# Four instruction lists of a software pipeline laid in a new order, and one wait of VectorE left out

## What is computed

```
h = jnp.maximum(_layernorm(x, axis=-1), 0.0)
x = x + _L0_gnn_ref(h, adj, ...)   # 4-head graph attention, a 1-head one, a feed-forward net, layernorm
h = jnp.maximum(_layernorm(x, axis=-1), 0.0)
x = x + _L1_gnn_ref(h, adj, ...)   # masked self-attention with 8 heads
h = jnp.maximum(_layernorm(x, axis=-1), 0.0)
x = x + _L2_gnn_ref(h, adj, ...)   # deg * (h @ Wi + b) + adj @ (h @ Wj)
h = jnp.maximum(_layernorm(x, axis=-1), 0.0)
x = x + _L3_gnn_ref(h, adj, ...)   # 1-head graph attention beside its own projection
```

## Time and profile before

| | before |
|---|---|
| median of 3 runs | 2682.44 us (2681.39 to 2683.78) |
| the profiled execution: its own time | 2683.62 us |
| its span, first to last instruction | 2681.8 us |
| mean granted clock of PE | 0.987 |
| PE busy | 2580.8 us, 96% of the span |
| PE's weight loads (PEld) busy | 2333.0 us, 87% |
| DVE busy | 2304.7 us, 86% |
| ACT busy | 2061.2 us, 77% |
| POOL busy | 1248.4 us, 47% |

### The profile page before, as it was taken

How to read it: one execution, slowest core, us unless ns; L and a number is a source line. 1 busy time by engine, 2 the same in 40 slices (tenths; PEclk the granted TensorE clock), 3 DMA queues, 4 the chain that set the end, 5 groups by cost and what they waited for, 6 DMA issues and landing times.

```text
span 2681.8 us, 64380 instructions
## 1 busy us (share of the span) xinstructions
PE 2580.8 (96%) x21761; PEld 2333.0 (87%) x21761; DVE 2304.7 (86%) x8352; ACT 2061.2 (77%) x5708; POOL 1248.4 (47%) x2015
## 2 busy tenths in 40 slices
PE   4899999999999999999999999999999999999985
PEld 3789999998998998999999999899999899999874
DVE  5689889889888888888888888888988988988884
ACT  4688788787787887877877877878878878878752
POOL 3545445444444444454454454454544544544431
PEclk9999999999999999999999999999999999999986
DMA  4000000000000000000000000000000000000000
GB/s 131 1 2 9 17 17 9 17 17 14 13 17 13 13 17 17 10 17 17 10 17 17 10 17 17 10 17 17 9 17 17 9 17 17 10 17 13 9 9 12
DMA packets 41286, 44.29 MB, mean 17 GB/s; under 512 B 2816, under 2 KB 40448, under 8 KB 40832
## 3 DMA queue, kind: packets, MB, share of 16 engines
q1 hardware_dynamic: 40816, 39.14, 4.6%
q10 hardware_dynamic: 144, 1.05, 0.1%
HBM read 23.40 MB, written 16.78 MB: 15 GB/s over the span
## 4 chain that ended last, share of the span: by engine, by line
PE 70%; ACT 20%; POOL 4%; issue 3%; DVE 2%; SPq 1%; DMA 0%; ACTq 0%; DVEq 0%; POOLq 0%
PE pA L1084 12%; PE pB L1191 11%; PE pE L1084 7%; PE pB L1158 7%; PE pB L1084 7%; ACT probs L579 7%; PE pF L1315 4%; PE pC L1084 3%; ACT pA L573 3%; ACT B_h_high L613 2%; PE pF L1328 2%; PE pA L1302 2%; PE pC L1237 2%; ACT C_hid_t L649 2%; ACT whs L560 1%
## 5 line engine op out<-in xcount | busy, mean ns | idle before, releaser
L677 ACT ACTIVATE F_s_t<-F_s_t,F_m 128x128 f32<-128x128 f32 x1024 | 325.3, 395 | 0.9 <-DVE F_m L863 0.8
L1191 PE MATMUL pB<-wout_high,B_h_high 128*128 128x258 f32 x1024 | 307.4, 300 | 1.1 <-DVE B_h_low L897 1.1
L1191 PE MATMUL pB<-wout_low,B_h_high 128*128 128x258 f32 x1024 | 289.6, 283 | 0.0
L1191 PE MATMUL pB<-wout_high,B_h_low 128*128 128x258 f32 x1024 | 288.8, 282 | 0.0
L1158 PE MATMUL pB<-probs,whs 128*128 128x128 f32 x2048 | 285.4, 282 | 1.4 <-ACT wh L620 1.1
L1158 PEld LDWEIGHTS pB<-probs,whs 128*128 128x128 f32 x2048 | 254.2, 192 | 20.8 <-issue 2.4
L1084 PE MATMUL pA<-wh_high,A_hT_high 128*128 128x512 f32 x512 | 229.0, 447 | 9.5 <-POOL wh_low L388 8.4
L889 DVE SCALAR_TENSOR_TENSOR B_e<-B_e,pB 128x512 f32<-128x512 f32 x256 | 172.9, 675 | 71.7 <-ACT B_e L605 71.4
L464 POOL TENSOR_TENSOR B_h_low<-B_e,B_h_high 128x512 fp32r<-128x512 f32 x128 | 165.8, 1295 | 111.8 <-ACT B_h_high L613 111.8
L1084 PE MATMUL pA<-wh_high,A_hT_low 128*128 128x512 f32 x512 | 202.9, 396 | 0.0
L1084 PE MATMUL pA<-wh_low,A_hT_high 128*128 128x512 f32 x512 | 202.7, 396 | 0.0
...
## 6 DMA issues: line engine op xcount, KB each, us to landing
...
```

The lines of the kernel that those rows point to most:

```text
L677: last = act.activation(F_s_t[:, s, h, :], F_s_t[:, s, h, :], ACT.Exp, scale=-1.0, bias=F_m[:, s, h:h + 1])
L1191: last = pe.matmul(pB[:, 0, 0:D + 2], a, w[:, k, :], start=(k == 0 and i == 0), stop=(k == KH - 1 and i == 2))
```

## The change

The four lists are written anew, and `x_there` loses its wait for `A_moments`. No computation is added, taken away or cut differently. Most steps keep their place in the pipeline and move by some places in the list; the lists also begin at another step, which by itself changes nothing. The diff (of the lists, which are tables, a line of each):

```diff
 PE_ORDER = """
-E_am:6 B_ol.1:2 C_hT:3 F_o:5 F_rT:5 D_v:4 C_hid:3 A_s.0:1 E_zT3:6 B_oh.1:2 A_wh_hi.1:1 F_out:5 A_s.1:1 E_h:6 C_ffn:3
+A_zT:1 A_pT.1:2 B_wh3.1:3 E_s:7 F_s:5 B_ol.0:2 E_pT:7 C_fT:3 A_f:1 E_o:7 C_s:3 A_wh_hi.0:1 B_oh.0:2 E_zT:6 A_wh_lo.0:1
...
 POOL_ORDER = """
-A_fleft:3 A_fright:3 A_rstd:2 E_right:9 E_rstd3:8 C_hb:5 C_low:5 B_lowh.1:4 D_xb:6 E_fcopy:8 E_rstd:7 C_xb:2 C_fcopy:4
-C_rstd:5 E_xb:7 D_rstd:5 B_lowh.0:3
+E_rstd3:9 C_low:6 E_fcopy:9 C_xb:4 B_lowh.1:5 E_rstd:8 E_xb:8 C_fcopy:5 C_rstd:6 D_rstd:6 B_lowh.0:4 E_right:9
+A_fleft:3 A_rstd:2 A_fright:3 D_xb:6 C_hb:5
...
             def x_there(g, p):
 
-                before(dve, "A_moments", g - 1)
                 dve.wait_ge(x_loaded, 16 * (p + 1))
```

More of the change, by code:

```diff
@@ L24 @@
 PE_ORDER = """
-E_am:6 B_ol.1:2 C_hT:3 F_o:5 F_rT:5 D_v:4 C_hid:3 A_s.0:1 E_zT3:6 B_oh.1:2 A_wh_hi.1:1 F_out:5 A_s.1:1 E_h:6 C_ffn:3
-B_wh0.1:2 D_q:4 B_wh1.1:2 A_pT.0:1 E_fT:6 B_wh2.1:2 A_pT.1:1 E_s:6 B_wh3.1:2 A_zT:0 F_s:4 B_ol.0:1 E_pT:6 C_fT:2 A_f:0
-E_o:6 C_s:2 B_oh.0:1 E_zT:5 A_wh_hi.0:0 A_wh_lo.0:0 C_pT:2 E_m.0:5 F_pTa.0:4 B_wh0.0:1 B_wh1.0:1 C_o:2 A_wh_lo.1:0
-F_pTb.0:4 D_zT:3 F_pTa.1:4 E_m.1:5 B_wh2.0:1 B_wh3.0:1 F_pTb.1:4 D_k:3
+A_zT:1 A_pT.1:2 B_wh3.1:3 E_s:7 F_s:5 B_ol.0:2 E_pT:7 C_fT:3 A_f:1 E_o:7 C_s:3 A_wh_hi.0:1 B_oh.0:2 E_zT:6 A_wh_lo.0:1
@@ L29 @@
+C_pT:3 F_pTa.0:5 B_wh0.0:2 E_m.0:6 C_o:3 F_pTb.0:5 B_wh1.0:2 A_wh_lo.1:1 E_m.1:6 B_wh2.0:2 F_pTa.1:5 B_wh3.0:2 D_zT:4
+F_pTb.1:5 C_hT:3 E_am:6 B_ol.1:2 D_k:4 F_rT:5 F_o:5 A_s.0:1 C_hid:3 D_v:4 E_zT3:6 A_wh_hi.1:1 B_oh.1:2 F_out:5 A_s.1:1
+E_h:6 B_wh0.1:2 C_ffn:3 D_q:4 A_pT.0:1 E_fT:6 B_wh1.1:2 B_wh2.1:2
 """.split()
 ACT_ORDER = """
-A_whc_lo.0:1 B_highh.0:2 E_mjhigh.0:6 F_pTca.0:5 F_expb.1:5 F_pTcb.0:5 D_high:4 C_oexp.0:3 C_oexp.1:3 E_mjhigh.1:6
-B_whc.0:2 F_pTca.1:5 F_pTcb.1:5 D_kc:4 C_hhigh:3 A_whc_lo.1:1 B_negl.1:2 F_high:5 B_expl.1:2 C_hidc:3 A_leaky.0:1
@@ L33 @@
[L33 to L36, removed]
+E_leaky:7 B_whc.1:3 E_exp.0:7 E_exp.1:7 E_attn:7 B_negl.0:2 B_expl.0:2 A_fround:1 C_leaky:3 F_expa.0:5 B_highl.0:2
+C_exp.0:3 E_high:6 C_exp.1:3 B_negh.0:2 F_expb.0:5 B_exph.0:2 C_attn:3 F_expa.1:5 A_whc_hi.0:1 E_mjhigh.0:6
@@ L37 @@
+A_whc_lo.0:1 B_highh.0:2 F_expb.1:5 C_oexp.0:3 C_oexp.1:3 F_pTca.0:5 F_pTcb.0:5 E_mjhigh.1:6 B_whc.0:2 D_high:4
+F_pTca.1:5 C_hhigh:3 F_pTcb.1:5 A_whc_lo.1:1 B_negl.1:2 B_expl.1:2 D_kc:4 A_leaky.0:1 F_high:5 C_hidc:3 B_highl.1:2
+A_exp.0:1 C_high:3 E_hT3:6 A_whc_hi.1:1 B_negh.1:2 B_exph.1:2 A_leaky.1:1 E_hc:6 B_highh.1:2 A_exp.1:1 A_attn.0:1
+D_qc:4 A_high:0 A_attn.1:1
 """.split()
 DVE_ORDER = """
-F_maxb.0:5 C_max.0:3 A_frest:1 C_max.1:3 B_hl.0:2 E_low:6 C_x1.1:4 F_maxb.1:5 B_lowl.0:2 D_stats.0:4 D_moments.0:4
@@ L40 @@
[L40 to L44, removed]
@@ L45 @@
-C_stats.1:3 C_g.0:3 E_z.0:5 C_moments.1:3 E_max.0:6 E_max.1:6 C_g.1:3 A_low:0 F_maxa.0:4 F_maxa.1:4 C_fTc:2 E_recip:6
-E_z.1:5 E_left.0:6 E_left.1:6 C_x1.0:3
+B_lowl.1:3 F_x2:6 A_recip.0:2 E_stats.0:6 A_norm.0:2 B_hh.1:3 E_stats.1:6 A_max.1:2 E_moments.0:6 A_z.1:1 C_y:4
+E_moments.1:6 A_recip.1:2 C_stats.0:4 A_norm.1:2 C_moments.0:4 C_stats.1:4 E_fTc:7 E_z.0:6 E_z.1:6 C_g.0:4 A_stats.0:0
+C_moments.1:4 A_low:1 E_max.0:7 E_max.1:7 F_maxa.0:5 F_maxa.1:5 E_recip:7 C_fTc:3 F_maxb.0:5 E_left.0:7 E_left.1:7
@@ new lines @@
+B_hl.0:2 C_g.1:4 A_frest:1 C_max.0:3 C_x1.0:4 C_max.1:3 F_maxb.1:5 B_lowl.0:2 E_low:6 C_x1.1:4 F_suma.0:5 D_stats.0:4
+D_stats.1:4 D_moments.0:4 B_hh.0:2 D_moments.1:4 F_suma.1:5 A_moments.0:0 C_recip:3 E_mjlow.0:6 E_mi.0:6 F_sumb.0:5
+A_stats.1:0 F_sumb.1:5 D_z.0:4 C_min:3 D_z.1:4 E_mjlow.1:6 C_h.0:3 A_moments.1:0 E_mi.1:6 C_h.1:3 F_recip:5 D_low:4
+F_rb:5 E_x3:6 E_stats3.0:6 E_stats3.1:6 A_z.0:0 E_moments3.0:6 E_moments3.1:6 C_hlow:3 F_rTc:5 F_on:5 E_z3.0:6
+B_hl.1:2 E_z3.1:6 A_max.0:1 F_low:5 D_vc:4
```

## The result

The changed kernel is slower: **2699.23 us**, the median of four runs (2697.1 to 2701.53), against 2683.11 for the kernel before beside it (four runs, 2681.39 to 2683.84). The ratio is 1.0064, with a 95% interval from 1.0052 to 1.0076. I had forecast 2664 us, with 2690 as the upper end.

A forecast was written before the change was run, and what follows sets the result against it. PE's own list was taken to bound the kernel. 2683.6 - 23.0 + 6.5 - 2 = 2665.1 us for the profiled execution, 1.2 above the median, gave a forecast of 2664 us, range 2652 to 2690.

The forecast's parts named there:

- VectorE's and GpSimd's passes kept apart: On DVE, both `E_z` no longer run beside POOL's `C_xb`; saves DVE about 1 us a round, PE doesn't wait: 0.
- The wait of `E_fT` goes: On PE before `E_fT`: with `E_hc` ahead of `A_exp.1` the wait, 0.39 us a round, goes; 59 rounds, -23.0 us.
- What is late next: On PE, thin margins as at `B_ol.0` and `A_wh_lo.1`: about one more just-in-time start a round, 0.11 us, +6.5 us.
- The wait in `x_there`: On DVE, the wait for moments of the pair before never held anything: 0.
- The start: First rounds, `wh_low` first on POOL: `A_wh_hi.0` wins 3 us, first `A_max` 2; -2 us, between -9 and +3.
- The end: End of the kernel: the same steps in other places, sign unknown; 0, within 5 us.
- POOL comes late: Rival: POOL late at `E_rstd`, DVE stands still, `E_pT` and F late; round 0.31 us longer, 2702 us; chance 0.15.
- The wait moves: Rival: `B_ol.0` or `E_pT` on PE waits as `E_fT` did; 0.3 to 0.45 given back, 2678 to 2687 us; chance 0.18.
- the sign of an error: PE idle before L1157 or L1212, DVE idle before `E_z` with POOL named, or a round of 39.9 us and more.

The follow-up runs named there:

- the two versions without the hold on PE's way: Changed kernel with `A_z.0` moved behind `C_hlow` on DVE, 2661.43 us; changed kernel with `C_hb` moved behind `E_rstd3` on POOL, 2648.88 us.

## Why the prediction was wrong

- **The step that failed** is *VectorE's and GpSimd's passes kept apart*, which I set at **0**. I looked at the one pair that I knew from the trace before, `E_z.0` beside `C_xb`, found it parted, and did not lay the rest of the new lists side by side. There `A_z.0` meets `D_xb` and `C_hb`. Measured: 0.78 us a round on PE at `C_hid` and 0.10 at `B_oh.1`, which is nearly the whole of the 0.89 by which moving `C_hb` alone shortens the round; taking the collision off PE's way gave 2699.23 - 2661.43 = 38 us by DVE's list, where `D_vc` is still late, and 2699.23 - 2648.88 = 50 by POOL's. The sentence "PE doesn't wait for it" was true of DVE's load as a whole and false of `C_hlow` and `D_vc`.
- In the other direction the same 0 was also wrong. Without `C_xb` out of `E_z.0`'s way, `E_hc`'s new place is worth 0.055 a round at most, and both together 0.325.
- *The wait of `E_fT` goes, -23.0*: right in mechanism, mis-sized. It gave 0.295 a round and not 0.39, because `A_pT.0` to `E_fT` takes 0.53 us without a wait; the 0.44 that I took came from `A_pT.1` and `E_s`, whose step is shorter. 59 rounds times 0.295 are 17.4 us.
- *What is late next, +6.5*: not there. With the hold off PE's way the round is 39.58 or 39.44; less the 0.295, other steps are 0.08 or 0.22 shorter in sum. The difference between these two, 0.14, is `B_oh.1` behind `D_vc`. Most of the other changes lie where the step that follows is another than before; which edit gives them was not taken apart.
- *The wait in `x_there`, 0*: right. *The start, -2*: `A_wh_hi.0` at 25.83 was forecast near 25, and the first `A_max` won 1.2. To pair 6 the changed kernel loses 2.3 us, inside the bounds of -9 to +3; but this is no measure of the order, since the run with `C_hb` ahead of `D_xb` wins 2.6 there with the hold in it, and the two versions without the hold on PE's way win 2.6 and 2.9. *The end, 0 within 5*: -5.6, and what gives it is open.
- Of the rivals, *POOL comes late* gave 2702 and stands nearest in time, but not for its reason: POOL was not late before `E_z`, DVE did not stand still there, and no wait of E or F was the cost. Its price, a pass of one engine held for a whole pass of the other, was the right kind; its place was `A_z.0` and `C_hlow`. *The wait moves* looked at `B_ol.0` and `E_pT`, which do not wait. What I had written as the sign of an error, a round of 39.9 and more, came; PE's idle time was before L1083, not before L1157 or L1212.
